# Adding a pair's four expert rows one after another through a PSUM bank, and a shorter run of identity products

## What is computed

```python
cw = (one_hot(topk_idx, E) * topk_w[..., None]).sum(1)   # 4 experts of 16 per token
act = silu(einsum('nh,eih->nei', xf, Wg)) * einsum('nh,eih->nei', xf, Wu)
y = einsum('nei,ne,ehi->nh', act, cw, Wd)                # sum over a token's 4 experts
shared = silu(xf @ Ws_g.T) * (xf @ Ws_u.T) @ Ws_d.T
x = layernorm(x + (x + y + shared))
```

## Time and profile before

| | us |
|---|---|
| median of three runs | 547.52 (547.26 to 547.93) |
| the profiled execution | 549.26 |
| its span, first to last instruction | 547.5 |
| PE busy in the span | 517.2 (94%) |
| DVE busy | 415.6 (76%) |
| ACT busy | 375.6 (69%) |
| POOL busy | 328.9 (60%) |

### The profile page before, as it was taken

One profiled execution on the slowest core, in us unless ns is written; L12 is line 12 of the kernel. 1 busy time (PEld: TensorE's weight loads), 2 busy tenths in 40 slices (PEclk: granted clock), 3 DMA queues, 4 the chain that ended last, 5 costly groups with the idle time before them and its releaser, 6 DMA issues.

```text
span 547.5 us, 11730 instructions
## 1 busy us (share of the span) xinstructions
PE 517.2 (94%) x3157; PEld 443.2 (81%) x3157; DVE 415.6 (76%) x1111; ACT 375.6 (69%) x961; POOL 328.9 (60%) x361
## 2 busy tenths in 40 slices
PE   5998899999999999999998999999999999999893
PEld 4687486686877868778676899999999999999692
DVE  3888598897997979989796847544344578979965
ACT  3694967848668486683745467777777787877453
POOL 4321113127657476576877777777777777777710
PEclk9999999999999999999999999999999999999998
DMA  7994403224233342312399868986766899997797
GB/s 162 306 270 161 164 38 117 78 83 140 72 137 108 122 142 73 135 71 99 108 299 393 264 232 257 307 262 192 221 206 209 280 291 339 348 319 261 264 338 248
DMA packets 70151, 111.06 MB, mean 203 GB/s; under 512 B 12260, under 2 KB 53477, under 8 KB 69576
## 3 DMA queue, kind: packets, MB, share of 16 engines
q1 hardware_dynamic: 56856, 74.36, 43.3%
q0 software_dynamic: 12672, 35.67, 17.5%
q10 hardware_dynamic: 560, 0.27, 0.2%
HBM read 61.63 MB, written 49.69 MB: 203 GB/s over the span
## 4 chain that ended last, share of the span: by engine, by line
PE 69%; DVE 12%; ACT 6%; issue 5%; DMA 5%; POOL 2%; SPq 0%; POOLq 0%; ACTq 0%; DVEq 0%
PE psum L792 8%; PE psum L733 6%; PE psum L735 6%; PE psum L734 6%; PE psum L986 6%; PE psum L988 6%; PE psum L987 6%; PE psum L970 5%; PE psum L862 4%; PE psum L767 3%; PE psum L1010 3%; PE psum L1011 3%; PE psum L1012 3%; PE psum L996 3%; DVE xc L1452 2%
## 5 line engine op out<-in xcount | busy, mean ns | idle before, releaser
L665 POOL DMA_INDIRECT x_buf<-row,row_id x128 | 129.0, 1008 | 51.3 <-issue 35.0
L657 POOL TENSOR_TENSOR m<-xc,zs 128x512 f32<-128x512 f32 x32 | 41.4, 1314 | 94.1 <-DVE shift L1530 55.1
L986 PE MATMUL psum<-ew_gu_hi,t_hi 128*128 x286 | 83.6, 292 | 0.4 <-issue 0.4
L988 PE MATMUL psum<-ew_gu_hi,t_lo 128*128 x286 | 80.8, 283 | 0.0
L987 PE MATMUL psum<-ew_gu_lo,t_hi 128*128 x286 | 80.8, 282 | 0.0
L1452 DVE SCALAR_TENSOR_TENSOR xc<-psum,cw_taps,xc 128x511 f32<-128x511 f32 (+2 forms) x96 | 70.7, 739 | 7.4 <-ACT halo_x L1121 6.0
L722 POOL DMA_INDIRECT y_buf<-y_out,y_ids x56 | 59.4, 1061 | 16.9 <-issue 15.4
L2058 DVE TENSOR_TENSOR e_act<-g_act,psum 128x512 f32<-128x512 f32 x36 | 24.5, 682 | 44.5 <-ACT g_act L1290 42.3
L792 PE MATMUL psum<-wout,m 128*128 128x256 f32 x256 | 57.3, 382 | 1.1 <-DVE m L1487 0.6
L733 PE MATMUL psum<-x_hi,win_hi 128*128 128x512 f32 x128 | 53.6, 419 | 3.6 <-DVE x_lo L1497 2.3
L792 PEld LDWEIGHTS psum<-wout,m 128*128 128x128 f32 x256 | 48.0, 190 | 10.0 <-DVE sp L1479 3.1
(11 more groups left out here) (256 smaller groups left out, 1396.1 us busy)
## 6 DMA issues: line engine op xcount, KB each, us to landing
tiles_in<-x_buf SPq DMA_DIRECT2D x143, 144.0 KB
y_pair<-y_buf SPq DMA_DIRECT2D x20, 512.0 KB
y_in<-y_buf SPq DMA_DIRECT2D x12, 512.0 KB, 6.6
xT<-in_x_T SPq DMA_DIRECT2D x8, 512.0 KB, 4.4
xtok<-in_x_tok SPq DMA_DIRECT2D x8, 512.0 KB, 3.5
gu_hi_buf<-w_hi_now SPq DMA_DIRECT2D x8, 512.0 KB, 2.9
x_buf<-pad_row SPq DMA_DIRECT2D x17, 144.0 KB
raw_gu<-in_wg_T SPq DMA_DIRECT2D x16, 128.0 KB, 3.2
```

Source lines behind the costliest of these rows:

```text
L665: nc.gpsimd.indirect_dma_start(out=x_buf, out_offset=bass.IndirectOffsetOnAxis(ap=row_id[t % ROWS][:, b, k:k + 1], axis=0), in_=row[t % RO ...
L986: pe.matmul(o, t_hi[par][:, k, r], w_hi, start=k == 0, stop=False)
L988: mm = pe.matmul(o, t_lo[par][:, k, r], w_hi, start=False, stop=k == KD - 1)
```

## The change

The four rows are no longer folded in half in place. `summed` is a view of PSUM bank 3 (512 elements per partition). `first_two` writes rows 0 + 1 of both blocks to it, in the place of `pair_half`; the new `third` adds row 2 behind `act_low` of the same quad; `sum_pair` adds row 3 and then adds the bank to `res`. The buffer is marked as free after row 3 was read. And `spin(20)` becomes `spin(8)`.

```diff
+        SUM_BANK = 3
...
-            spin(20)
+            spin(8)
             late_sums(LAST_BLOCKS)
...
+            summed = psum[:, SUM_BANK, :].rearrange("p (b d) -> p b d", d=D)
+            def first_two(i):
                 y = y_pair[i % 2]
                 at_least(dve, f"pair_in{i % 2}", 32 * (i // 2 + 1))
-                V.tensor_tensor(y[:, :, 0:2, :], y[:, :, 0:2, :], y[:, :, 2:4, :], ALU.add).then_inc(s["pair_halved"], 1)
+                V.tensor_tensor(summed, y[:, :, 0, :], y[:, :, 1, :], ALU.add).then_inc(s["pair_step"], 1)
+            def third(i):
+                at_least(dve, "pair_step", 2 * i + 1)
+                V.tensor_tensor(summed, y_pair[i % 2][:, :, 2, :], summed, ALU.add).then_inc(s["pair_step"], 1)
             def sum_pair(i):
-                y, x2 = y_pair[i % 2], res[:, 2 * i:2 * i + 2, :]
-                at_least(dve, "pair_halved", i + 1)
-                V.tensor_tensor(y[:, :, 0, :], y[:, :, 0, :], y[:, :, 1, :], ALU.add).then_inc(s["pair_added"], 1)
+                x2 = res[:, 2 * i:2 * i + 2, :]
+                at_least(dve, "pair_step", 2 * i + 2)
+                V.tensor_tensor(summed, y_pair[i % 2][:, :, 3, :], summed, ALU.add).then_inc(s[f"pair_used{i % 2}"], 1)
+                at_least_alone(dve, f"pair_used{i % 2}", i // 2 + 1)
+                V.tensor_tensor(x2, x2, summed, ALU.add).then_inc(s["pair_added"], 1)
                 at_least(dve, "pair_added", i + 1)
-                V.tensor_tensor(x2, x2, y[:, :, 0, :], ALU.add).then_inc(s[f"pair_used{i % 2}"], 1)
-                at_least_alone(dve, f"pair_used{i % 2}", i // 2 + 1)
...
                 if q in HALF_QUADS:
-                    pair_half(HALF_QUADS.index(q))
+                    first_two(HALF_QUADS.index(q))
                 late_first(q)
...
                 act_low(j, u)
+                if q in HALF_QUADS:
+                    third(HALF_QUADS.index(q))
                 late_last(q)
```

More of the change, by code:

```diff
@@ L231, in mamba_moe @@
             y_in0 y_in1 y_in2 y_in3 y_in4 y_in5 y_in6 y_in7 y_in8 y_in9 y_in10 y_in11 y_in12 y_in13 y_in14 y_in15
-            pair_in0 pair_in1 pair_halved pair_added pair_used0 pair_used1 y_paired y_total
+            pair_in0 pair_in1 pair_step pair_added pair_used0 pair_used1 y_paired y_total
             cut_done
@@ L401, in mamba_moe @@
         SPARE_BANK = 6
+        SUM_BANK = 3
+        assert all(a < b for a, b in zip(SUM_QUADS[:-1], HALF_QUADS[1:])) and LATE_TABLE + 1 < HALF_QUADS[0]
         def dt_bank(t, c):
@@ L2063, in act_low @@
                 V.tensor_tensor(a_lo[:, :], psum[:, 4, :], f32(a_hi[:, :]), ALU.subtract).then_inc(s["a_l"], 1)
-            def pair_half(i):
+            summed = psum[:, SUM_BANK, :].rearrange("p (b d) -> p b d", d=D)
+            def first_two(i):
                 y = y_pair[i % 2]
                 at_least(dve, f"pair_in{i % 2}", 32 * (i // 2 + 1))
-                V.tensor_tensor(y[:, :, 0:2, :], y[:, :, 0:2, :], y[:, :, 2:4, :], ALU.add).then_inc(s["pair_halved"], 1)
+                V.tensor_tensor(summed, y[:, :, 0, :], y[:, :, 1, :], ALU.add).then_inc(s["pair_step"], 1)
+            def third(i):
+                at_least(dve, "pair_step", 2 * i + 1)
+                V.tensor_tensor(summed, y_pair[i % 2][:, :, 2, :], summed, ALU.add).then_inc(s["pair_step"], 1)
             def sum_pair(i):
-                y, x2 = y_pair[i % 2], res[:, 2 * i:2 * i + 2, :]
-                at_least(dve, "pair_halved", i + 1)
-                V.tensor_tensor(y[:, :, 0, :], y[:, :, 0, :], y[:, :, 1, :], ALU.add).then_inc(s["pair_added"], 1)
+                x2 = res[:, 2 * i:2 * i + 2, :]
[3 more added lines that the diff above has]
+                V.tensor_tensor(x2, x2, summed, ALU.add).then_inc(s["pair_added"], 1)
                 at_least(dve, "pair_added", i + 1)
-                V.tensor_tensor(x2, x2, y[:, :, 0, :], ALU.add).then_inc(s[f"pair_used{i % 2}"], 1)
-                at_least_alone(dve, f"pair_used{i % 2}", i // 2 + 1)
                 for b in range(2 * i, 2 * i + 2):
@@ L2283, in _ @@
             for i in range(len(SUM_QUADS), BLOCK_PAIRS):
-                pair_half(i)
+                first_two(i)
+                third(i)
                 sum_pair(i)
```

## The result

| | before | changed |
|---|---|---|
| median of 20 runs | 548.01 us | 545.83 us |
| lowest and highest | 546.14, 549.66 | 544.47, 551.8 |
| span of the profiled execution | 547.5 us | 544.4 us |

The ratio of the times is **0.9967, 95% interval 0.9954 to 0.998**: faster by 0.33%, some 1.8 us by the ratio, 2.2 by the medians. The forecast was 4.0 us (543.5, range 541.8 to 546.5). The time is in the range and the direction is right; the gain is about half of the forecast, by the ratio somewhat less (1.8 of 4.0), by the medians somewhat more (2.2).

What follows compares the result with a forecast made beforehand. The prediction took POOL's late sends, then the last loads and DVE's additions, to set the end. PE's last sum ending at 535.5 instead of 539.5 gave 4.0 us, subtracted from the median 547.5: 543.5 us, range 541.8 to 546.5.

Steps and rivals of the forecast that it cites:

- What bounds the kernel: At the end, POOL's late sends, then the last loads and DVE's additions set the time; POOL's excess is 7.7 us.
- ten of ten: All ten 1,024-element DVE additions at L2069 lengthen a POOL send, by 0.47 to 0.79 us each, 6.5 us in sum.
- The sum for the changed kernel: PE's last sum ends at 535.5 instead of 539.5 us, 4.0 us gained; main case, chance 0.62.
- A send waits for an addition of two SBUF inputs, not for one with PSUM: A POOL send begun during DVE's two-SBUF-input addition waits until about 0.12 us before its end; one PSUM input doesn't block.
- The residue of 0.6 to 1.3 us: POOL's excess left after the change, from the one two-SBUF-input addition per pair; some 6.3 of 7.7 us goes.
- The two parts need each other: With twenty products the last four blocks' sums start at 534.3 instead of 531.65 us; gain some 1.7 us only.
- DVE on the path in quads 34 and 35: DVE's added work makes quad 34's `e_act` 0.4 us late and quad 35's 1.13 later in all; PE waits.
- rival 2: DVE additions through PSUM take 0.74 to 0.84 us, costing PE 0.1 to 0.4 in six quads: 545 to 546.5; chance 0.09.
- 3: Slower than before: DVE additions through PSUM take over 0.86 us, at 0.95 giving 549.7 us; chance 0.05.
- Rival 4: DVE's additions did not lengthen POOL's sends, so POOL ends where it did: 547.5 us; chance 0.07.
- rival 5: PE's clock falls to half in a pause ahead of the last sums, 1 to 2 us on the path: 545; chance 0.04.
- Rival 1: POOL's sends still collide, 3.5 us of excess stay and the loads set the end again: 544.5 us; chance 0.13.

Runs made afterwards that it cites:

- the sum in SBUF: The changed kernel's four additions in the same places, with the running sum in SBUF instead of PSUM, 8 products: 546.37 us, ratio 0.9972 against before.
- the third row's place: The changed kernel with the third row added ahead of `act_low` instead of behind it: 545.24 us, ratio 0.9952 against before.

## Why the prediction was half right

**What bounds the kernel: the step that failed.** The prediction read one execution of before and took its bound for the kernel's. That POOL's lateness sets the end and ten of ten additions meet a send was true of that execution. In four profiles of before the excess was 7.7, 8.9, 4.5 and 6.2 us. In the last two PE and the 20 products set the end, not POOL; there, the 3 to 5 us saved on POOL are worth nothing. Only in the first did the loads set it. The used profile had a sign of this: its 549.26 us stood 1.7 above the median then shown, and its span of 547.5 stands 1.2 above what the median of 548.0 leaves for a span (with the 1.7 to 1.8 us that lie outside it in every run). The prediction then subtracted a gain counted in that slow execution from the median ("the difference is taken from the median"), and so gave 543.5 both as the time and as a profiled span, between which 1.7 to 1.8 us lie in every run. Taken from 549.26, the gain of 4.0 gives 545.3 us; measured 545.83. The 1.7 us forecast for twenty products went wrong in the same way: from 549.26 they give 547.6, about the median of before, and measured was no gain (548.57, ratio 1.0006).

**The sum for the changed kernel: right.** Forecast was a span of 543.5; measured 544.4 and 542.9 in two profiles. Tail: 543.5 - 512.97 = 30.5 forecast, 30.4 and 30.5 measured. The last `down` was forecast at 512.97 and came at 513.96 and 512.43; the 1.5 us between the two are about what DVE waited for the pairs' loads in the first (0.88 and 0.56 at two places) and not in the second. Such waits were missing in the working. Counted against a typical execution of before (513.30 and 32.5), the same sum gives: tail 32.5 - 30.5 = 2.0 less, `e_act` of quad 35 later by 0.95 - 0.22 = 0.7, so 1.3 us; where POOL is in the end of before, more: 3.3 us against the second profile (34.5), 4.5 against the first (35.7). The ratio's 1.8 us lies between 1.3 and these, as it would for a mixture of such executions; how often each happens is not known from four profiles, so this is argued and not shown.

**A send waits for an addition of two SBUF inputs, not for one with PSUM: right**, shown by the sum in SBUF (4.1 against 1.0 and 1.5) and by the single sends. "Ten of ten", which stood for it in the prediction, holds in the first two profiles of before; in the third it was six, in the fourth eight. The residue of 0.6 to 1.3 us was measured at 1.5 and 1.0.

**The two parts need each other: half right.** The additions without the shorter run gain nothing (1.0006). But the shorter run alone gains 0.2% (0.998, an interval that barely leaves out 1), where taking the loads as before's bound left nothing to gain. Adding the rest brings it to 0.9967; the intervals overlap, so how much of the gain is POOL's is open: the two ratios differ by 0.13%. With the sum in SBUF, where POOL still loses 4.1 us, the gain is as large within the noise (0.9972).

**DVE on the path in quads 34 and 35: right**, by the wait of 0.95 us that went with the third row's place. Rivals 2 (slow additions through PSUM) and 3 fell with 684 to 696 ns; rival 2's own terms, six quads at 0.1 to 0.4 us on 543.5, give 544.1 to 545.9 and not the 545 to 546.5 that stand there. Rival 4 fell with the SBUF kernel, rival 5 with a granted clock of 1.00 from 530 to 538 us, the last sums among them (3.98 us for 16 records, of which 0.36 are waits for DVE). Rival 1 (loads at the end again) happened in no profile of the changed kernel.

## What to carry to other kernels

Where two chains end within a few microseconds of each other, one profile shows one winner: take several of the kernel before and look whether the last waits have the same names, and count the gain against each. Subtract a gain only from the execution in which it was counted, not from the median. A delay that depends on how two engines' rhythms meet (here 1.29 us of POOL against DVE's additions) is a property of an execution, not of the program. And before shortening an engine, ask what the next one needs from it: here POOL could lose 4 us at no measurable cost, while products that compute nothing stood on PE's path.

## What the runs showed of the hardware

- An indirect DMA issued on POOL that begins while DVE adds two SBUF operands takes up to 2.03 us instead of 0.98; with one operand in PSUM 0.98 or 0.99. Of 61 sends that began inside an addition of two SBUF operands in the four profiles of before, 57 took 0.985 us from 0.12 us before that addition's end on, each within 0.02 us; the other four are in the next point.
- In the other order neither loses: of 192 additions of two SBUF operands that began inside a running send (seven profiles) none took longer than usual, 0.70 us, or 1.23 in the form of 1,024 elements. Where an addition began 0.01 to 0.05 us ahead of a send, either can win: five such additions took 0.72 to 0.76 and the sends 0.98 or 0.99, two took 0.68 and the sends 1.49.
- A DVE addition of 128x512 fp32 with its output in PSUM takes 696 ns, with input and output there 684 to 690, as in SBUF.
- A pair's loads (0.5 MB each) came up to 3.09 us late for DVE in one execution (before, fourth) and not at all in another of the same kernel.
